# Three small moves at the seams of the expert layers: a first mean, a first turn, and every other high half

## The reference

```
h = x @ W_in + b_in                                  # 3125 x 256
for l in range(3):
    agg = segment_sum(h[src], dst) / max(deg, 1)
    logits = concat(h, agg) @ router_W[l] + router_b[l]     # 8 experts
    gates = softmax over the two largest, zero elsewhere
    weak   = relu(agg @ weak_W[l, e] + b)            # 4 experts, 256 -> 256
    strong = relu(agg @ strong_W1[l, e] + b1) @ strong_W2[l, e] + b2   # 4 experts, 256 -> 512 -> 256
    h = h + sigmoid(h @ conf_W[l] + conf_b[l]) * sum_e gates_e * expert_e
return h @ W_out + b_out
```

## Time and profile before

| | us |
|---|---|
| median of 3 runs | 3167.43 (3164.25 to 3170.72) |
| the profiled execution | 3162.65 |
| its span | 3160.1 |
| PE busy in it | 2940.7 (93%) |
| DVE busy | 2182.1 (69%) |
| ACT busy | 943.3 (30%) |
| mean granted TensorE clock | 0.982 of full |

### The profile page before, as it was taken

The page is one execution under the profiler, slowest core; times in us unless marked ns, Lnnn a source line. Parts: engine busy times, 40 slices in busy tenths (PEclk is TensorE's granted clock), DMA queues, the critical chain, the costliest instruction groups (busy, mean ns, idle before and its releaser), DMA issues. The chain is left out here.

```text
span 3160.1 us, 47679 instructions
## 1 busy us (share of the span) xinstructions
PE 2940.7 (93%) x18758; PEld 1775.9 (56%) x18758; DVE 2182.1 (69%) x4012; ACT 943.3 (30%) x1776; POOL 17.8 (1%) x23
## 2 busy tenths in 40 slices
PE   2888889999998999999989999989999999999997
PEld 2566555556454544544556666655666665666665
DVE  7999655557246777776667666777767677777676
ACT  3888521123211000000032222343323234223223
POOL 2000000000000000000000000000000000000000
PEclk8999999999999999999989999999999999999999
DMA  5455367776006554554330000020000002000001
GB/s 130 141 152 155 108 191 220 218 221 189 23 1 204 154 171 153 165 156 129 92 116 4 4 4 4 3 84 4 4 7 4 3 15 73 4 4 4 4 3 43
DMA packets 310959, 265.85 MB, mean 84 GB/s; under 512 B 32767, under 2 KB 289409, under 8 KB 308174
## 3 DMA queue, kind: packets, MB, share of 16 engines
q1 hardware_dynamic: 296558, 259.28, 27.0%
q10 hardware_dynamic: 13760, 2.61, 0.4%
q0 software_dynamic: 416, 0.85, 0.1%
HBM read 172.67 MB, written 90.05 MB: 83 GB/s over the span
## 5 line engine op out<-in xcount | busy, mean ns | idle before, releaser
L1931 PE MATMUL psum<-r_wd,room_a 128*128 128x512 fp8e4 (+1 forms) x2600 | 570.0, 375 | 0.8 <-ACT r_ht L286 0.8
L2509 PE MATMUL psum<-counts,m_h 128*128 128x512 fp8e4 (+2 forms) x2100 | 418.1, 355 | 13.2 <-DVE m_h L2224 7.9
L2573 PE MATMUL psum<-m_weights,x_nodes 128*128 128x256 f16 (+1 forms) x3600 | 414.4, 273 | 12.6 <-DVE m_wtmp L2332 10.2
L2554 PE MATMUL psum<-room_a,m_weights 128*128 128x512 f16 (+2 forms) x2016 | 411.5, 356 | 14.6 <-ACT x_nodes L2464 8.7
L1931 PEld LDWEIGHTS psum<-r_wd,room_a 128*128 128x128 f16 x2600 | 242.3, 97 | 296.0 <-ACT r_ht L286 0.9
L2573 PEld LDWEIGHTS psum<-m_weights,x_nodes 128*128 128x128 f16 (+1 forms) x3600 | 351.6, 99 | 64.7 <-DVE m_wtmp L2332 9.6
L2456 ACT ACTIVATE m_agg<-psum,x_nodes 128x512 f32<-128x512 f32 (+2 forms) x336 | 239.6, 718 | 292.7 <-PE psum L2554 289.9
L2509 PEld LDWEIGHTS psum<-counts,m_h 128*128 128x128 f16 x2100 | 206.0, 99 | 208.9 <-issue 12.4
L2554 PEld LDWEIGHTS psum<-room_a,m_weights 128*128 128x128 f16 x2016 | 193.8, 99 | 214.5 <-issue 40.2
L2476 ACT ACTIVATE m_hT<-m_hT,room_a 128x256 f32<-128x256 f32 x300 | 135.9, 501 | 553.5 <-DVE m_hT L2346 553.5
L2332 DVE SCALAR_TENSOR_TENSOR m_wtmp<-psum,x_nodes,room_a 128x256 f32<-128x256 f32 (+1 forms) x300 | 144.9, 483 | 136.7 <-PE psum L2573 135.4
(11 more groups left out here) (311 smaller groups left out, 3381.3 us busy)
## 6 DMA issues: line engine op xcount, KB each, us to landing
r_wd<-packed_sym SPq DMA_DIRECT2D x120, 640.0 KB, 4.1
packed_counts<-strip SPq DMA_DIRECT2D x21, 1800.0 KB, 7.8
sym_blocks<-packed_counts SPq DMA_DIRECT2D x88, 384.0 KB, 4.9
packed_sym<-sym_blocks SPq DMA_DIRECT2D x84, 384.0 KB, 3.5
w_stage<-in_L_gnn_strong_W SPq DMA_DIRECT2D x12, 1024.0 KB, 6.8
m_weights<-in_L_gnn_strong_W SPq DMA_DIRECT2D x21, 512.0 KB, 4.8
x_parked<-x_nodes SPq DMA_DIRECT2D x2, 1600.0 KB, 5.9
x_nodes<-x_parked SPq DMA_DIRECT2D x2, 1600.0 KB, 6.3
```

Of the source, the lines that this page charges most:

```text
L1931: m = pe.matmul(bank[pair[b]][:, 0:2 * cw], h16[:, part, p0 + i, :], f_[:, 2 * b:2 * b + 2, :], start=(p0 + i == 0 and part == 0), stop=(p ...
L2509: m = pe.matmul(bank[kb][:, 0:cw], h16[:, part, i, kb * P:(kb + 1) * P], A[:, i, c_:c_ + cw], start=(i == 0 and part == 0), stop=(i == NT ...
L2554: m = pe.matmul(bank[4 + hh % 2][:, 0:cw], w_[:, i, kb, f * P:(f + 1) * P], agg16[:, j, kb, 0:cw], start=(x_ == 0), stop=(x_ == len(todo) ...
L2573: m = pe.matmul(bank[b_][0:r_, 0:H], s_[:, pa[0] * BANK + k * P:pa[0] * BANK + k * P + r_], w_[:, pa[1], f, :], start=(f == 0 and pa == PA ...
```

## The change

1. In `dve_layer` the mean is split in two: `mean_block(0, 0)`, the first block of chunk 0 with its waits, is called in the loop of the splits, ahead of piece 7 of 10; the second block, and the low half, stay where `mean(0)` was.
2. In `pe_layer`, in layer 0 alone, `turn(0)` is called behind the spreading of the largest value instead of ahead of it.
3. In the last chunk ACT writes the high half only of even hidden blocks (f = 0 and 2). For odd ones DVE casts again, as in the other chunks, and ACT signals `s_kept` after its first activation.

```diff
--- before.py
+++ after.py
@@ -2162,6 +2162,10 @@
                 def hidden_at(l, ci, e, f):
                     return (l * NCH + ci) * HIDDENS + e * FB + f
 
+                def high_by_act(ci, f):
+
+                    return ci == NCH - 1 and f % 2 == 0
+
                 def mixed_at(l, ci, e, k):
 
                     return NSG * tiles_done(l, ci) + e * len(tiles_of(CH[ci])) + k
@@ -2233,15 +2237,21 @@
                             vec.scalar_tensor_tensor(flat[:, 1, c_], loaded_piece(k)[:, c_], scale_of(l, n_, wsc), flat[:, 0, c_], ALU.mult,
                                                      ALU.subtract).then_inc(w_low, 1)
 
-                    def mean(ci):
+                    def mean_block(ci, kb):
                         n = l * NCH + ci
                         c_, cw = CH[ci]
-                        vec.wait_ge(inv_in, 16 * (n + 1))
-                        if n:
-                            vec.wait_ge(s_split, HIDDENS * n)
-                        for kb in range(KB):
-                            vec.wait_ge(e_summed, KB * n + kb + 1)
-                            vec.scalar_tensor_tensor(agg[:, kb, 0:cw], bank[kb][:, 0:cw], sc[:, 3:4], invd[:, 0:cw], ALU.mult, ALU.mult).then_inc(e_mean, 1)
+                        if kb == 0:
+                            vec.wait_ge(inv_in, 16 * (n + 1))
+                            if n:
+                                vec.wait_ge(s_split, HIDDENS * n)
+                        vec.wait_ge(e_summed, KB * n + kb + 1)
+                        vec.scalar_tensor_tensor(agg[:, kb, 0:cw], bank[kb][:, 0:cw], sc[:, 3:4], invd[:, 0:cw], ALU.mult, ALU.mult).then_inc(e_mean, 1)
+
+                    def mean(ci, blocks=range(KB)):
+                        n = l * NCH + ci
+                        c_, cw = CH[ci]
+                        for kb in blocks:
+                            mean_block(ci, kb)
                         vec.wait_ge(e_mean_high, n + 1)
                         vec.scalar_tensor_tensor(agg16[:, 1, :, 0:cw], agg[:, 0:KB, 0:cw], sc[:, 1:2], agg16[:, 0, :, 0:cw], ALU.mult,
                                                  ALU.subtract).then_inc(e_mean_low, 1)
@@ -2317,7 +2327,7 @@
                             if loc >= NSH:
                                 ci0, e0 = (loc - NSH) // HIDDENS, (loc - NSH) % HIDDENS // FB
                                 vec.wait_ge(s_mixed, mixed_at(l, ci0, e0, len(tiles_of(CH[ci0])) - 1) + 1)
-                            if ci < NCH - 1:
+                            if not high_by_act(ci, f):
                                 vec.tensor_copy(s_[:, 0:cw], wide32).then_inc(steps.handle, steps.up())
                                 settle()
                             vec.tensor_tensor(s_[:, BANK:BANK + cw], wide32, s_[:, 0:cw], ALU.subtract).then_inc(s_split, 1)
@@ -2352,6 +2362,9 @@
                                 vec.wait_ge(k_added, NWK * t + e + 1)
 
                     for k in range(NPC):
+
+                        if k == NPC - 3:
+                            mean_block(0, 0)
                         split_low(k)
                     vec.wait_ge(mrw_in, MRW_IN)
                     if l == 0:
@@ -2367,7 +2380,7 @@
                     vec.tensor_scalar(b1s[:], b1[:, l], ks[:, 1:2], None, ALU.mult).then_inc(steps.handle, steps.up())
                     settle()
                     mark["h_bias", l] = steps.n
-                    mean(0)
+                    mean(0, range(1, KB))
                     for ci in range(NCH):
                         more = ci + 1 < NCH
                         ts = tiles_of(CH[ci])
@@ -2591,10 +2603,14 @@
                                                   start=(y_ == 0), stop=(y_ == len(todo) - 1))
                                 m.then_inc(k_mixed, 1)
 
-                    turn(0)
+
+                    if l:
+                        turn(0)
 
                     pe.wait_ge(steps.handle, mark["h_max", l])
                     pe.matmul(bank[7][:, 0:P], sc[:, 0:1].to_broadcast([P, P]), ident[:], start=True, stop=True).then_inc(max_spread, 1)
+                    if l == 0:
+                        turn(0)
                     edges(0)
                     ROUTE_IN = 12
                     per = ROUTE_IN // len(tiles_of(CH[0]))
```

## The result

The changed kernel takes 3172.85 us (median of 16 runs, 3166.58 to 3177.52), the kernel before 3167.70 beside it (16 runs). The ratio is 1.0019, with a 95% interval of 1.0012 to 1.0025, that is 3.8 to 7.9 us slower. I had forecast +1.9 us; the sign is right, the size is three times too small by this measurement, and the median lies 0.05 us outside my range.

A forecast was written before the change was run, and what follows sets the result against it. TensorE was taken as the bound, with gains only where it idles at layer starts and last chunks. Wait +2.1, clock +1.6, layers 1 and 2 -1.4, turn 0, last chunks -0.4 gave +1.9: 3169.3 us, range 3164.2 to 3172.8.

The forecast's parts named there:

- The mean's wait in layer 0: Layer 0's start: DVE waits 2.7 us at the early mean for the inverse degrees' load; layer loses 2.1 us.
- The gain in layers 1 and 2: Starts of layers 1 and 2: early mean without a wait, routing weights load 0.68 us earlier in each.
- the price of the clock in layer 0: Layer 0's start: granted clock falls to 0.50 after 3.5 us of PE idle, costing 1.6 us.
- the sum: Whole kernel: wait +2.1, clock +1.6, layers 1 and 2 -1.4, turn 0, last chunks -0.4, together +1.9 us.
- The last chunks: Last chunk of each layer: odd blocks' casts back on DVE, -0.12 us a layer, -0.4 in all.
- the slow rival: Last chunks: longer PE idle makes the clock fall in layers 0 and 2 too; +5.2 us, chance 0.18.
- The turn: Layer 0's start: first turn behind the largest value brings nothing; bounds -0.2 and +0.2 us.
- The cases: Whole kernel: forecast 0.45, clock kept in layer 0 0.17, no wait there 0.15, slow by last chunks' clock 0.18, unnamed 0.05.

The follow-up runs named there:

- mean_inverses_first: Against the kernel before: early first mean alone, with each layer's first row of inverse degrees loaded at the head of SP's queue; ratio 0.9992.
- mean_from_layer1: Against the kernel before: early first mean in layers 1 and 2 alone, nothing else changed; ratio 0.9991.
- edges_inverses: Whole change with inverse degrees loaded first and all 24 edge matmuls ahead of the four routing tiles; ratio 0.9998 to the kernel before.
- highs_alone: Against the kernel before: every other high half of the last chunk cast by DVE, nothing else changed; ratio 1.0015.
- after_again: The changed kernel once more, for a second profile and more times; ratio 1.0010 to the kernel before.
- highs_shift4: Odd high halves of the last chunk on DVE, plus four unread matmuls before each layer's first hidden block; ratio 1.0015 to the kernel before.
- before_again: The kernel before, unchanged, measured once more beside itself; ratio 1.0003.

## Why the prediction was wrong

- **The mean's wait in layer 0** was right: DVE idle at the mean until the DMA lands, 2.36 us for 2.7, splits and scales late behind it, the routing 1.7 us late for 2.1. mean_inverses_first and mean_from_layer1 show that it is the load and layer 0 alone. The gain in layers 1 and 2 was 0.8 each for 0.68 by the early mean alone; in the whole change layer 2 keeps 0.5 of it.
- **The step that failed** is the price of the clock in layer 0, "the price is the same work twice ... so 1.6 us". That was read from a stretch of dense matmuls in the last chunk, where the low clock lasted about 3 us of busy work. In the routing it lasted ten, and cost 4.4 us in the first profile and nearly 7 in the second (from the first routing matmul to the first hidden one 13.97 us for 7.11 before). Put 4.4 in place of 1.6 and the sum is +4.7, inside the measured interval; that it fits so well is luck, for the sum leaves out other falls of like size. Between the profiles of before and of changed the three starts differ by +6.1, -0.8 and +4.4 us, the six long chunks by -3.3, -0.1 and +1.6, the last chunks by +1.1, -2.0 and -0.5: +6.4 in all. Why the low clock lasts so long in the routing was not tested alone; in edges_inverses it falls behind routing tiles in a row with no idle just ahead of them.
- **The last chunks** were right without the clock (-0.3 to -0.5 a chunk for -0.12; cast 323 ns for 320, idle 3.05 for 3.0), and the slow rival named the right place for what the third edit costs alone: highs_alone loses 4 us by falls behind that idle. Its condition was half right, "it decides from a stretch at which the clock no longer holds": at the timing of before 3.05 us fell in layer 0 and 2.84 did not, but over all timings 2.84 us fell as often as 3.05, and a shift of 0.9 us ahead of it turned it round.
- **The turn** is 0, as worked out from ACT's queue: 38.5 us to the first hidden matmul against 38.6.
- **The cases** treated each fall as a separate coin. In fact a shift at the start of a layer changes the falls behind it, and the parts' effects by the ratios (+5, +5, 0 us) do not add to the whole's (+6, or +3 in its second measurement); the same change without the wait turns from slower to faster. That the places are fixed for a given start is shown for layer 0 alone; how the three layers hang together stays open.

## What to carry to other kernels

When an instruction is moved up, move with it in thought every wait that it carries, and read the landing time of each load it waits for: a transfer that was early enough for the old place can be the last in its queue for the new one. Then look at what the stalled engine's consumer does next; here the small matmuls behind an idle TensorE ran at the low clock for ten microseconds, and that cost two and a half times what the wait itself did (4.4 us and 1.7). And where differences of a few microseconds are in play, compare seams in several profiles with their granted clock before crediting an edit with them.

## What the runs showed of the hardware

- The granted clock fell to 0.50 not only behind idle stretches but also behind a stretch of 9-column matmuls with no idle just ahead of it (edges_inverses, layer 1: four routing tiles in 3.5 us, then 24 matmuls in 7.02 us instead of 5.34).
- It stayed at 0.50 through ten microseconds of routing and edge matmuls of which PE was busy 9.2 and 10.0 (changed, layers 0 and 2), and through 17 in two other profiles (after_again, layer 0; highs_shift4, layer 2).
- The places of the falls repeat between executions: in layer 0 at 250 and 390 us in eight of eight kernels with the same start, at neither place in the two that were shifted by 0.9 us. One such fall costs the six chunks 1.7 us: with none, one or two of them they take 417.8, 419.4 or 421.1 us.
- An unchanged kernel's timed runs spread from 3163 to 3177 us (before_again), more than any effect looked for here.
